# Scattering expert results to token order as each block ends, in a 16-expert stage on one Trainium2 core

## The chip, the cores and the metric

The kernel runs on one core of one Trainium2 chip. The metric is device time in microseconds (us) of one execution of the whole program; before the change it is 1019.32 us, the median of three runs (1016.58 to 1019.96).

## The reference, cut to what matters

The program is a chain of eight stages on 1024 tokens (4 sequences of 256) of 256 channels. The fourth of them is a mixture of experts: 16 experts of which each token uses two, and a shared expert that all use. Cut to that stage, with `x` the normalized tokens:

```python
probs = softmax(xt @ Wr.T + bias)
topk_val, topk_idx = top_k(probs, 2)
w = topk_val / (sum(topk_val) + 1e-9)
g = einsum('th,ehi->tei', xt, Wg)          # 16 experts, h = 256, i = 128
u = einsum('th,ehi->tei', xt, Wu)
y = einsum('tei,eih->teh', silu(g) * u, Wd)
oh = one_hot(topk_idx, 16)
routed = einsum('tke,tk,teh->th', oh, w, y)
shared = silu(xt @ sWg) * (xt @ sWu) @ sWd
```

The result, times a gate, is added to the token stream.

## The kernel before, in words

The kernel computes only the two chosen experts of each token. `sparse_moe` (L1279) first routes: VectorE finds each token's two experts and, with counts from TensorE, gives each of the 2048 (token, choice) pairs a slot. The slots of one expert are padded to whole blocks of 128, so there are NB = 31 blocks at most; `sloti` holds the slot of each pair. A product with one-hot matrices (L1425) turns this around: for each block and each of its 128 rows it gives the token's place within its tile (`ps[:, 6, 0:32]`) and the tile number (`ps[:, 6, 32:64]`), from which L1571 and L1572 make `rowid`.

The normalized tokens are stored to `h_rows` in HBM (L1333). POOL then issues one indexed DMA per block (L1352), which gathers 128 rows of 1 KB into one of NG = 4 buffers `xg`. A gather waits until TensorE has turned the block that used the buffer before (`s_xTp`).

The blocks run as a pipeline written out by hand. In step i TensorE turns block i (`turn_rows`, L1435), multiplies block i-1 with its expert's gate and up weights (`gate_up`, L1446), turns the hidden rows of block i-2 (L1455) and multiplies those of block i-3 with the down weights (L1468). ScalarE copies the turned rows (L1382) and takes silu (L1389). VectorE multiplies gate and up (`gated`, L1578), copies the turned hidden rows (`keep_hidden`, L1586), and copies the block's result rows into one of NY = 4 buffers `yo` (`keep_rows`, L1593). Between these, VectorE quantizes the weights of a later stage (L983 to L1002, 16 pieces). After the 31 blocks the same steps run for the NS = 8 token tiles of the shared expert, whose results VectorE adds to `x` at once (`add_shared`, L1598).

SP stores each block's result rows to `y_rows` in HBM (L1337) in the order of slots; `keep_rows` waits for the store of four blocks before (`s_st`). When all 31 stores have landed, POOL issues 16 more gathers (L1358), one per token tile and choice, which bring the two result rows of each token into `yk`. VectorE then adds them, each times its weight (L1617, L1619), tile by tile in the order of the gathers.

At the end of its list TensorE turns the quantized weights (`turn_w5`, L1031, L1037) and ScalarE copies them out of PSUM (`keep_w5`, L1043, L1045). The next stage starts when all engines have come to the end of this one.

Order within an engine is the order of the program; `v.link` issues a VectorE instruction and waits for it, `v.mark` issues it alone. Semaphores go up by 16 per DMA.

Of the kernel before, what the change touches and what calls it, by code (L numbers as in the profile page):

```python
# [10 lines left out]
P = 128  # L11
B, S, D, C = 4, 256, 256, 128
T = B * S
NT = T // P
# [6 lines left out]
ALU = mybir.AluOpType  # L21
ACT = mybir.ActivationFunctionType
AX = mybir.AxisListType
F32 = mybir.dt.float32
BF16 = mybir.dt.bfloat16
U16 = mybir.dt.uint16
U32 = mybir.dt.uint32
I32 = mybir.dt.int32
# [23 lines left out]
def build(nc, a, out):  # L52
    with ExitStack() as ctx:
        def sb(name, shape, dt=F32):
            return ctx.enter_context(nc.sbuf_tensor(name, shape, dt))
# [4 lines left out]
        def sem(name):  # L60
            held.append(nc.alloc_semaphore(name=name))
            return held[-1]
# [10 lines left out]
        ps = ctx.enter_context(nc.psum_tensor("ps", [P, 8, 512], F32))  # L73
# [10 lines left out]
        iota = sb("iota", [P, P])  # L84
        pcol = sb("pcol", [P, 1])
# [9 lines left out]
        g8 = sb("g8", [P, 8])  # L95
        rt3, rt7 = sb("rt3", [P, KD, 16]), sb("rt7", [P, KD, 8])
        h_rows = nc.dram_tensor("h_rows", (T, D), F32).ap()
        y_rows = nc.dram_tensor("y_rows", (31 * P, D), F32).ap()
        bias3 = sb("bias3", [P, 16])
        WORDS_B = WORDS_C = 13056  # L100
        low = ExitStack()
# [908 lines left out]
        def load_w5(sp, raw5):  # L1010
            sp.dma_start(raw5[:, 0, :], a["L2_W1"]).then_inc(s_w5, 16)
            sp.dma_start(raw5[:, 1, :], a["L2_W2"]).then_inc(s_w5, 16)
# [266 lines left out]
        def sparse_moe(tag, E, F, NB, W, WE, router, gate_col, s_weights, loads, ar, shared=False, bias=None,  # L1279
# [6 lines left out]
            NG, NY = 4, 4  # L1286
# [12 lines left out]
            sloti, blki = ar.take([2, NT], I32), ar.take([2, NT], I32)  # L1299
# [1 line left out]
            ohb = ar.take([NR, 32])  # L1301
            tokr = ar.take([NR, 2, 32], BF16)
            low_id = ar.take([32])
            rowid = ar.take([32], U32)
            le = ar.take([32, E])
            eb, ebi = ar.take([32]), ar.take([32], I32)
            xg = ar.take([NG, D])
# [3 lines left out]
            yo = ar.take([NY, D])  # L1311
            yk = ar.take([2, NT, D])
# [7 lines left out]
                 "xTp xT gu sil itm iTp iT y yo x").split())  # L1320
            s_got = [sem(f"{tag}_got{i}") for i in range(NG)]
            s_st = [sem(f"{tag}_stored{i}") for i in range(NY)]
            s_yk = [sem(f"{tag}_yk{i}") for i in range(NT)]
            over = lambda v: v.unsqueeze(2).broadcast_to([P, NT, E])
            xrows = out.rearrange("b (h p) d -> p (b h) d", p=P)
            with nc.Block(tag) as block:
                @block.sync
                def _(sp):
                    if with_w5:
                        load_w5(sp, raw5)  # L1330
                    for i in range(2):
                        sp.wait_ge(s_h, NT // 2 * (i + 1))
                        sp.dma_start(h_rows.rearrange("(t p) d -> p t d", p=P)[:, i * NT // 2:(i + 1) * NT // 2, :],  # L1333
                                     h[:, i * NT // 2:(i + 1) * NT // 2, :]).then_inc(s_hrow, 16)
                    for b in range(NB):
                        sp.wait_ge(s_yo, b + 1)
                        sp.dma_start(y_rows[b * P:(b + 1) * P, :], yo[:, b % NY, :]).then_inc(s_st[b % NY], 16)  # L1337
                    if store:
                        for hf in range(2):
                            sp.wait_ge(s_x, NS + TPH * (hf + 1))  # L1340
                            sp.dma_start(xrows[:, hf * TPH:(hf + 1) * TPH, :],
                                         x[:, hf * TPH:(hf + 1) * TPH, :]).then_inc(s_out, 16)
                        sp.wait_ge(s_out, 32)

                @block.gpsimd
                def _(pool):
                    pool.wait_ge(s_hrow, 32)
                    pool.wait_ge(s_rid, 1)
                    for b in range(NB):
                        if b >= NG:  # L1350
                            pool.wait_ge(s_xTp, b - NG + 1)
                        nc.gpsimd.indirect_dma_start(xg[:, b % NG, :], None, h_rows,  # L1352
                                                     bass.IndirectOffsetOnAxis(rowid[:, b:b + 1], 0)).then_inc(s_got[b % NG], 16)
                    for j in range(NY):
                        pool.wait_ge(s_st[j], 16 * len(range(j, NB, NY)))
                    for t in range(NT):
                        for k in range(2):
                            nc.gpsimd.indirect_dma_start(yk[:, k, t, :], None, y_rows[0:NB * P, :],  # L1358
                                                         bass.IndirectOffsetOnAxis(sloti[:, k, t:t + 1].bitcast(U32), 0)
                                                         ).then_inc(s_yk[t], 16)  # L1360

                def block_banks(u):

# [125 lines left out]
                def _(dve):  # L1489
                    v = Steps(dve, s_v)  # L1490
                    norm_on_vector(dve, v, s_var, s_sd, s_h)
                    nc.vector.tensor_scalar(tri[:, :], iota[:, :], pcol[:, 0:1], None, ALU.is_gt).then_inc(s_unit, 1)
                    nc.vector.memset(ones[:, :], 1.0).then_inc(s_unit, 1)
                    nc.vector.memset(unit, 1.0).then_inc(s_unit, 1)

# [61 lines left out]
                    for k in range(2):  # L1557
                        o = slice(k * NT, (k + 1) * NT)
                        ins = nc.vector.tensor_tensor(tokr[:, o, 1, :], ohb[:, o, :],
                                                      iota[:, 0:NT].unsqueeze(2).broadcast_to([P, NT, 32]), ALU.mult)  # L1560
                    ins.then_inc(s_tokr, 1)
                    for k in range(2):
                        nc.vector.tensor_tensor(ohr[:, k * NT:(k + 1) * NT, :], iota[:, :].unsqueeze(1).broadcast_to([P, NT, P]),
# [4 lines left out]
                    v.link(nc.vector.tensor_reduce(eb, le, AX.X, ALU.add))  # L1568
                    nc.vector.tensor_scalar(ebi, eb, float(E - 1), float(WE), ALU.min, ALU.mult).then_inc(s_eb, 1)
                    dve.wait_ge(s_inv, 1)  # L1570
                    v.link(nc.vector.tensor_copy(low_id, ps[:, 6, 0:32]))  # L1571
                    nc.vector.scalar_tensor_tensor(rowid, ps[:, 6, 32:64], float(P), low_id, ALU.mult, ALU.add).then_inc(s_rid, 1)  # L1572

                    def gated(u):
                        dve.wait_ge(s_sil, u + 1)
# [35 lines left out]
                        if with_w5:  # L1611
                            quantize_w5(dve, v, i, raw5, wq5, tmp5, am5, s_wq)
                    for t in range(NT):
                        dve.wait_ge(s_yk[t], 32)
                        if shared:
                            dve.wait_ge(s_x, t + 1)
                        v.link(nc.vector.scalar_tensor_tensor(x[:, t, :], yk[:, 0, t, :], wk[:, t, 0:1], x[:, t, :],  # L1617
                                                              ALU.mult, ALU.add))
                        nc.vector.scalar_tensor_tensor(x[:, t, :], yk[:, 1, t, :], wk[:, t, 1:2], x[:, t, :],  # L1619
                                                       ALU.mult, ALU.add).then_inc(s_x, 1)  # L1620

        def stage3():
            sparse_moe("stage3", NE3, P, NB3, W3, UW3, rt3, 5, s_w3, 7, Arena(regA, regC), shared=True, bias=bias3,
                       with_w5=True)
# [722 lines left out]
```

## Time and profile before

| | us |
|---|---|
| median of 3 runs | 1019.32 |
| lowest and highest run | 1016.58, 1019.96 |
| the profiled execution, its own time | 1017.64 |
| its span in the trace | 1015.9 |
| VectorE busy in the span | 728.4 (72%) |
| TensorE matmuls busy | 675.2 (66%) |
| ScalarE busy | 331.4 (33%) |
| POOL busy | 193.8 (19%) |

The span is the time from the first to the last instruction of the profiled execution. Busy times are sums over all eight stages, each of which has another limit, so they don't say what the stage in question is worth; that is read from the trace of its own stretch, 441 to 542 us. An indexed DMA on POOL shows as a busy POOL while its descriptors are made; the data lands later. PE is TensorE, DVE VectorE, ACT ScalarE, and SPq the queue of SP's DMAs.

### The profile page before, as it was taken

The numbers are of one execution on the slowest core, as the hardware profiler recorded it, in microseconds if no ns is written. First come the engines' busy times: TensorE is split into PE (matmuls) and PEld (weight loads), VectorE is DVE, ScalarE is ACT, GpSimd is POOL, SyncE is SP. The second block draws the span as 40 slices with busy tenths as digits, with TensorE's granted clock in tenths as the row PEclk, the third lists the DMA queues.
The fourth block names the chain that finished last, engine by engine and source line by source line (L and its number), as shares of the span: only waits on it lengthen the run. The fifth ranks groups of instructions, "written<-read, shape, count | busy, mean of one in ns | idle before, by whom it ended". The sixth has DMA issues, their size and how long they took to land. (4 is left out here: it accounts for less than half of the span.)

```text
span 1015.9 us, 9504 instructions
## 1 busy us (share of the span) xinstructions
PE 675.2 (66%) x3066; PEld 442.1 (44%) x3069; DVE 728.4 (72%) x1418; ACT 331.4 (33%) x530; POOL 193.8 (19%) x167
## 2 busy tenths in 40 slices
PE   4418986777777354349963454999990344389997
PEld 2304543343343243335742243556550123277775
DVE  5987798999999767659653783766429886944554
ACT  4004424525350133122302324555530222423231
POOL 0000002212222000034352940000003132203342
PEclk9759999999999776569986855999995575569999
DMA  9200004555555840323632000000005000000000
GB/s 243 76 12 0 1 0 78 87 94 93 97 90 97 206 128 1 124 62 108 133 92 87 0 1 0 1 2 1 1 1 207 0 1 0 10 0 1 20 3 21
DMA packets 35746, 55.27 MB, mean 54 GB/s; under 512 B 4578, under 2 KB 23658, under 8 KB 34418
## 3 DMA queue, kind: packets, MB, share of 16 engines
q0 software_dynamic: 10960, 22.94, 12.5%
q1 hardware_dynamic: 24738, 31.73, 10.2%
q8 instruction: 25, 0.41, 0.2%
q14 instruction: 23, 0.19, 0.1%
HBM read 31.73 MB, written 6.16 MB: 37 GB/s over the span
## 5 line engine op out<-in xcount | busy, mean ns | idle before, releaser
L499 PE MATMUL ps<-hT,regA 128*128 128x512 f32 x256 | 116.8, 599 | 1.3 <-ACT hT L424 1.3
L669 POOL DMA_DIRECT2D yssm<-regB x32 | 38.7, 1210 | 294.6 <-DVE regB L621 210.8
L613 DVE TENSOR_TENSOR_SCAN regB<-regB 128x512 f32<-128x512 f32 x64 | 74.9, 1212 | 5.0 <-DVE regB L608 0.5
L510 PE MATMUL ps<-regA,regC 128*128 128x256 f32 x256 | 64.8, 398 | 20.5 <-DVE regC L628 17.2
L1914 PE MATMUL ps<-regC 128*34 128x256 f32 x256 | 68.2, 389 | 11.6 <-ACT regC L1794 11.6
L499 PEld LDWEIGHTS ps<-hT,regA 128*128 128x128 f32 x256 | 49.2, 193 | 52.2 <-issue 47.7
L510 PEld LDWEIGHTS ps<-regA,regC 128*128 128x128 f32 x256 | 49.7, 199 | 39.8 <-DVE regC L628 27.1
L434 ACT ACTIVATE regC<-ps 128x512 f32<-128x512 f32 x32 | 19.1, 597 | 138.1 <-PE ps L499 138.0
L1128 POOL TENSOR_TENSOR w_lo<-regA,w_hi 128x768 fp32r<-128x768 f32 x22 | 42.4, 1932 | 100.3 <-ACT w_hi L1090 100.3
L1352 POOL DMA_INDIRECT regA<-h_rows,regA x31 | 29.5, 951 | 137.4 <-DVE regA L1572 107.1
L1266 DVE TENSOR_TENSOR regB<-regB,ps 128x512 f32<-128x512 f32 x22 | 15.1, 687 | 45.9 <-ACT regB L1108 45.9
L2036 DVE RECIPROCAL regC<-ps 128x8 f32<-128x8 f32 x32 | 6.6, 207 | 57.4 <-PE ps L1922 57.3
L1794 ACT ACTIVATE regC<-ps 128x512 f32<-128x512 f32 x64 | 38.1, 596 | 26.4 <-PE ps L1900 25.3
L621 DVE TENSOR_TENSOR regB<-regB,ps 128x512 f32<-128x512 f32 x64 | 41.1, 684 | 6.9 <-DVE regB L613 6.4
L456 PE MATMUL ps<-regC 96*128 96x512 bf16 x64 | 23.0, 387 | 31.7 <-DVE regB L621 19.8
L408 ACT ACTIVATE regB<-regC 128x510 f32<-128x510 f32 x64 | 40.2, 707 | 6.0 <-DVEq L647 5.9
L1858 PE MATMUL ps<-ident,regA 128*128 128x128 f32 x192 | 29.4, 318 | 17.7 <-DVE regA L2012 13.6
L608 DVE TENSOR_TENSOR regB<-regC,ps 128x512 f32<-128x512 f32 x64 | 40.9, 680 | 0.0
L2021 DVE TENSOR_REDUCE regC<-ps 128x4 f32<-128x960 f32 x64 | 40.3, 685 | 0.0
L2114 POOL TENSOR_TENSOR h<-h,regB 128x512 f32<-128x512 f32 x4 | 5.2, 1291 | 181.8 <-DVE h L156 181.8
L173 PE MATMUL ps<-ident,h 128*128 128x128 f32 x112 | 19.7, 350 | 28.0 <-DVE h L156 27.2
L1914 PEld LDWEIGHTS ps<-regC 128*34 128x34 f32 x256 | 23.6, 112 | 33.8 <-ACT regC L1794 12.5
(365 smaller groups left out, 1701.7 us busy)
## 6 DMA issues: line engine op xcount, KB each, us to landing
yssm<-regB POOLq DMA_DIRECT2D x32, 512.0 KB, 5.0
regB<-in_L_w SPq DMA_DIRECT2D x4, 1088.0 KB, 12.1
regA<-in_L_w SPq DMA_DIRECT2D x1, 4224.0 KB, 14.9
y_rows<-regA SPq DMA_DIRECT2D x31, 128.0 KB
regB<-in_L_w SPq DMA_DIRECT2D x1, 2176.0 KB, 13.1
regC<-in_L_W SPq DMA_DIRECT2D x2, 1024.0 KB, 5.7
x<-in_x SPq DMA_DIRECT2D x1, 1024.0 KB, 5.7
regB<-in_L_gate_pk SPq DMA_DIRECT2D x1, 1024.0 KB, 8.0
```

Source lines behind the costliest of these rows:

```text
L408: nc.scalar.activation(dA[:, g % RD, k, :, 1:S], src, ACT.Exp, scale=alog[:, k, n:n + 1]).then_inc(s_dA, 1)
L499: m = nc.tensor.matmul(ps[:, 2 + 2 * (u % 2) + j, :], w[:, k * 2048 + c * P:k * 2048 + (c + 1) * P], hT[:, k, hf * HALF:(hf + 1) * HALF], ...
L510: m = nc.tensor.matmul(ps[:, t // 2, (t % 2) * D:(t % 2 + 1) * D], itm[:, u % 2, t * P:(t + 1) * P], WDv[:, c // 2, c % 2, :], start=(c == ...
L608: v.mark(nc.vector.tensor_tensor(dBu[:, k, :], half(du, k, hf), ps[:, 6, :], ALU.mult))
L613: v.mark(nc.vector.tensor_tensor_scan(hs[:, k, :], dA[:, g % RD, k].rearrange("p b l -> p (b l)"), dBu[:, k, :], 0.0, ALU.mult, ALU.add))
L621: ins = nc.vector.tensor_tensor(hc[:, g % 2, k, :], hs[:, k, :], ps[:, 7, :], ALU.mult)
L669: nc.gpsimd.dma_start(y, hc[:, g % 2], accum_op=ALU.add).then_inc(s_y, 16)
L1128: nc.gpsimd.tensor_tensor(wP[LO][:, u % RING, :], W[:, u % NC, :], wP[HI][:, u % RING, :].bitcast(F32), ALU.subtract).then_inc(s_wL, 1)
L1352: nc.gpsimd.indirect_dma_start(xg[:, b % NG, :], None, h_rows, bass.IndirectOffsetOnAxis(rowid[:, b:b + 1], 0)).then_inc(s_got[b % NG], 16)
L1794: nc.scalar.activation(prob[:, n % 4, :], ps[:, 4 + n % 2, :], ACT.Exp, scale=SCALE4).then_inc(s_p, 1)
L1914: m = nc.tensor.matmul(ps[0:VW, 6 + j % 2, (n % 2) * S:(n % 2 + 1) * S], vaug[:, 2 * b + kt, hd, :], prob[:, n % 4, kt * S:(kt + 1) * S], ...
L2021: nc.vector.tensor_reduce(dst[:, :, :, j], sc[:, :, :, lo:hi], AX.X, ALU.max, negate=True).then_inc(s_mx, 1)
```

## The change

Result rows no longer go to slot order and come back by gathers. Each block's rows are written by an indexed DMA on POOL straight to a row that belongs to the token and choice: `y_rows` gets 2 x 1024 further rows, first those of choice 0 in token order, then those of choice 1. Rows of a block that no token uses go to a row of the old part. The tile number that the one-hot product carries is therefore counted from NB (31) up, plus 8 for the second choice, so that it is also the target's row number divided by 128, and 0 marks an unused row. Six VectorE instructions make from it `outid` (the target row) and `rowid` (the token, by masking).

POOL's list now holds both kinds of indexed DMA: gather i, then, from i = 8 on, the scatter of block i - 8, which waits for `keep_rows` of that block. SP stores nothing in the blocks; it waits until all scatters have landed and issues eight plain loads of two token tiles each, choice 0 and 1 in turn. VectorE waits for one pair of loads per two tiles.

```diff
-        y_rows = nc.dram_tensor("y_rows", (31 * P, D), F32).ap()
+        y_rows = nc.dram_tensor("y_rows", (31 * P + 2 * T, D), F32).ap()
...
-            rowid = ar.take([32], U32)
+            rowid, outid = ar.take([32], U32), ar.take([32], U32)
+            slot_f, slot_i, unused, spare = ar.take([32]), ar.take([32], I32), ar.take([32]), ar.take([32])
...
-            s_yk = [sem(f"{tag}_yk{i}") for i in range(NT)]
+            s_yk = [sem(f"{tag}_yk{i}") for i in range(NT // 2)]
...
-                    for b in range(NB):
-                        sp.wait_ge(s_yo, b + 1)
-                        sp.dma_start(y_rows[b * P:(b + 1) * P, :], yo[:, b % NY, :]).then_inc(s_st[b % NY], 16)
+                    for j in range(NY):
+                        sp.wait_ge(s_st[j], 16 * len(range(j, NB, NY)))
+                    for i in range(NT // 2):
+                        for k in range(2):
+                            r = NB * P + k * T + 2 * i * P
+                            sp.dma_start(yk[:, k, 2 * i:2 * i + 2, :],
+                                         y_rows[r:r + 2 * P, :].rearrange("(t p) d -> p t d", p=P)).then_inc(s_yk[i], 16)
...
-                    for b in range(NB):
-                        if b >= NG:
-                            pool.wait_ge(s_xTp, b - NG + 1)
-                        nc.gpsimd.indirect_dma_start(xg[:, b % NG, :], None, h_rows,
-                                                     bass.IndirectOffsetOnAxis(rowid[:, b:b + 1], 0)).then_inc(s_got[b % NG], 16)
-                    for j in range(NY):
-                        pool.wait_ge(s_st[j], 16 * len(range(j, NB, NY)))
-                    for t in range(NT):
-                        for k in range(2):
-                            nc.gpsimd.indirect_dma_start(yk[:, k, t, :], None, y_rows[0:NB * P, :],
-                                                         bass.IndirectOffsetOnAxis(sloti[:, k, t:t + 1].bitcast(U32), 0)
-                                                         ).then_inc(s_yk[t], 16)
+                    LAG = 2 * NG
+                    for i in range(NB + LAG):
+                        if i < NB:
+                            if i >= NG:
+                                pool.wait_ge(s_xTp, i - NG + 1)
+                            nc.gpsimd.indirect_dma_start(xg[:, i % NG, :], None, h_rows,
+                                                         bass.IndirectOffsetOnAxis(rowid[:, i:i + 1], 0)
+                                                         ).then_inc(s_got[i % NG], 16)
+                        if i >= LAG:
+                            b = i - LAG
+                            pool.wait_ge(s_yo, b + 1)
+                            nc.gpsimd.indirect_dma_start(y_rows, bass.IndirectOffsetOnAxis(outid[:, b:b + 1], 0),
+                                                         yo[:, b % NY, :], None).then_inc(s_st[b % NY], 16)
...
+                    v.link(nc.vector.tensor_scalar(spare, iota[:, 0:32], float(P), pcol[:, 0:1], ALU.mult, ALU.add))
...
                         ins = nc.vector.tensor_tensor(tokr[:, o, 1, :], ohb[:, o, :],
-                                                      iota[:, 0:NT].unsqueeze(2).broadcast_to([P, NT, 32]), ALU.mult)
+                                                      iota[:, NB + k * NT:NB + (k + 1) * NT].unsqueeze(2)
+                                                      .broadcast_to([P, NT, 32]), ALU.mult)
...
-                    v.link(nc.vector.tensor_copy(low_id, ps[:, 6, 0:32]))
-                    nc.vector.scalar_tensor_tensor(rowid, ps[:, 6, 32:64], float(P), low_id, ALU.mult, ALU.add).then_inc(s_rid, 1)
+                    v.link(nc.vector.scalar_tensor_tensor(unused, ps[:, 6, 32:64], 0.0, spare, ALU.is_equal, ALU.mult))
+                    v.link(nc.vector.tensor_tensor(low_id, ps[:, 6, 0:32], unused, ALU.add))
+                    v.link(nc.vector.scalar_tensor_tensor(slot_f, ps[:, 6, 32:64], float(P), low_id, ALU.mult, ALU.add))
+                    v.link(nc.vector.tensor_scalar(slot_i, slot_f, float(-NB * P % T), None, ALU.add))
+                    v.mark(nc.vector.tensor_copy(outid, slot_f))
+                    nc.vector.tensor_scalar(rowid.bitcast(I32), slot_i, T - 1, None, ALU.bitwise_and).then_inc(s_rid, 1)
+                    v.settle()
...
-                        dve.wait_ge(s_yk[t], 32)
+                        dve.wait_ge(s_yk[t // 2], 32)
```

## Rows read from the trace of the kernel before

**Rows 1.** Stretches: length, busy of each engine (instructions), granted clock, DMA share, GB/s.

```profile
452.00:482.00 30.00, 27.15 (x120) 17.23 (x118) 28.94 (x83) 8.44 (x26) 12.28 (x13) 1.00 0.40 111
482.00:500.00 18.00, 17.01 (x86) 12.81 (x86) 12.14 (x39) 6.22 (x19) 8.75 (x10) 1.00 0.63 131
500.00:512.00 12.00, 12.00 (x65) 10.20 (x64) 6.42 (x24) 3.71 (x12) 0.69 (x1) 1.00 0.59 122
```

**Rows 2.** Line L1352, the gathers of the blocks: durations, and what POOL waited for.

```profile
L1352 POOL DMA_INDIRECT regA<-h_rows,regA x31: 942/944/1079, 440.9 to 499.7; - x31
...
  PE ps L1435: 27.5, 23
```

**Rows 3.** Timeline of POOL: gathers 8, 29 and 30, and the first closing gather.

```profile
452.41 0.94 POOL L1352 DMA_INDIRECT regA<-h_rows,regA  x1 [0.90 <-PE ps L1435]
...
498.12 0.94 POOL L1352 DMA_INDIRECT regA<-h_rows,regA  x1 [0.68 <-PE ps L1435]
499.75 0.94 POOL L1352 DMA_INDIRECT regA<-h_rows,regA  x1 [0.68 <-PE ps L1435]
514.78 0.94 POOL L1358 DMA_INDIRECT regA<-y_rows,regA  x1 [14.09 <-DMA y_rows<-regA]
```

**Rows 4.** Line L1358, the closing gathers: durations, and idle time between them.

```profile
L1358 POOL DMA_INDIRECT regA<-y_rows,regA x16: 942/946/1132, 514.8 to 533.8; - x16
...
  issue: 4.6, 15
```

**Rows 5.** Timeline of the closing sum and of the end of the stage.

```profile
525.17 0.48 DVE L1617 SCALAR_TENSOR_TENSOR x<-regA,x 128x256 f32<-128x256 f32 x1
...
526.08 0.48 DVE L1617 SCALAR_TENSOR_TENSOR x<-regA,x 128x256 f32<-128x256 f32 x1
...
537.08 0.48 DVE L1619 SCALAR_TENSOR_TENSOR x<-regA,x 128x256 f32<-128x256 f32 x1
537.59 1.86 ACT L1043 COPY W1q<-ps 128x2048 bf16<-128x2048 bf16 x1 [17.76 <-remote]
539.35 1.87 ACT L1045 COPY W2q<-ps 128x2048 bf16<-128x2048 bf16 x1
```

**Rows 6.** Waits between 400 and 545: total us, times, longest.

```profile
ACT W1q L1043 <- remote: 17.8, 1, 17.8
...
DVE x L1617 <- DMA regA<-y_rows,regA: 4.7, 3, 1.7
...
DVE x L1598 <- PE ps L1468: 3.4, 2, 1.8
```

**Rows 7.** Timeline: the transposes that the first ScalarE copy reads.

```profile
523.19 1.06 PE L1031 MATMUL ps<-identb,regC 128*128 128x128 bf16 x16
```

**Rows 8.** Timeline of the head: row numbers, first gather, first use of it.

```profile
439.58 0.18 DVE L1571 COPY regA<-ps 128x32 f32<-128x32 f32 x1
439.80 0.19 DVE L1572 SCALAR_TENSOR_TENSOR regA<-ps,regA 128x32 uint32<-128x32 f32 x1
440.88 1.08 POOL L1352 DMA_INDIRECT regA<-h_rows,regA  x1 [107.11 <-DVE regA L1572]
...
443.86 0.69 PE L1435 MATMUL ps<-ident,regA 128*128 128x128 f32 x2 [5.06 <-DMA regA<-h_rows,regA]
```

**Rows 9.** SP's stores (line L1337), and two loads: KB each, us to landing.

```profile
L1337 SPq DMA_DIRECT2D y_rows<-regA x31: 319/320/333, 452.8 to 512.3; - x31
...
x<-in_x SPq DMA_DIRECT2D x1, 1024.0 KB, 5.7
...
regD<-in_q_wkv SPq DMA_DIRECT2D x1, 256.0 KB, 2.8
```

**Rows 10.** POOL's plain DMA out of SBUF in an earlier stage, and its landing.

```profile
L669 POOL DMA_DIRECT2D yssm<-regB x32: 1192/1201/1467, 154.8 to 332.6; - x32
...
DMA to landing us min/median/max: 5.0/5.0/5.6
```

**Rows 11.** Timeline: block 30 turned, a product and two result copies behind it.

```profile
505.60 0.38 PE L1435 MATMUL ps<-ident,regA 128*128 128x128 f32 x2
...
507.20 0.29 DVE L1578 TENSOR_TENSOR regA<-regA,ps 128x128 f32<-128x128 f32 x1 [0.67 <-ACT regA L1389]
...
507.60 0.41 DVE L1593 COPY regA<-ps 128x256 f32<-128x256 f32 x1
...
511.82 0.41 DVE L1593 COPY regA<-ps 128x256 f32<-128x256 f32 x1
```

## The prediction

> **What bounds the kernel now.** I read the table of stretches first, then the two groups of indexed DMAs on POOL, then the timeline of the stage's three seams (first gather, last block, closing sum).
>
> The 16-expert stage runs 31 expert blocks between about 441 and 512 us. While the second-layer weights are quantized beside the blocks, VectorE is full: 28.94 of 30 us. Later TensorE is: 17.01 of 18, then 12.00 of 12, at a granted clock of 1.00 [rows 1]. POOL is never full. Its 31 gathers take 0.94 us each, and it sits idle 27.5 us over 23 waits for TensorE to free a row buffer [rows 2]. From gather 8 (452.41) to gather 30 (499.75) the 22 blocks take 47.34 us, 2.15 a block [rows 3]; the last two gathers are 1.63 apart.
>
> After the blocks POOL waits 14.09 us for the last stored block and starts the closing gathers at 514.78 [rows 3]. These are 16 instructions of 0.946 us with 4.6 us of idle time over 15 gaps, so one every 1.25 us: POOL's own pitch with nothing to wait for [rows 4]. VectorE starts the weighted sum at 525.17, at 0.91 us a tile (to 526.08), and ends at 537.57 instead of after eight such tiles, because it waits 4.7 us for gathers [rows 5, 6]. Only then, at 537.59, does ScalarE copy the turned weights; both copies end at 541.22 and the stage closes [rows 5]. TensorE's transposes for the first copy stand at 523.19 to 524.25 [rows 7]. What kept ScalarE 17.8 us is given only as "remote" [rows 6].
>
> **The change, part by part.**
>
> *Head.* The two instructions after the inverse permutation become six, linked, before the row numbers are ready. Links stand 0.22 us apart (439.58 to 439.80) [rows 8], so four more cost 0.9 us. POOL's first gather and everything behind it wait for this: +0.9. The extra instruction beside the constants runs while VectorE waits for the router's logits: nothing, at worst 0.2. The token matrices keep their sizes: nothing.
>
> *Blocks.* SP's 31 stores leave a queue that did nothing else (0.32 us each [rows 9]): no gain on the path. POOL gets 31 scatters. From gather 8 on it alternates gather i and scatter i-8. A scatter's cost isn't in this trace. The nearest row is the gather: same 128 rows of 1 KB, indices on the other side. I take its 1.25 pitch. The upper bound is POOL's plain DMA from SBUF, 1.20 us long [rows 10], pitch 1.50. The lower bound is that POOL never binds.
>
> At 1.25 a pair needs 2.50 us where a block took 2.15, so POOL becomes the bound. Gather 8 moves to 453.3 (the head's 0.9), and gather 30 starts at 453.3 + 22 x 2.50 = 508.3 instead of 499.75. Before, gather 30 had slack: the first gather ends at 441.96 and TensorE uses it at 443.86, so 1.9 us to use [rows 8]. Gather 30 was therefore usable at 499.75 + 0.94 + 1.9 = 502.6 and TensorE took it at 505.60 [rows 11]. After, it is usable at 508.3 + 2.84 = 511.1: block 30 moves by 5.5 us. The eight shared tiles behind it keep their pace, so the start of the sum moves from 525.17 to 530.7.
>
> *The scatter's landing and the wait on it.* VectorE's copy into the ring of four result buffers now waits for the scatter of four blocks before. If gather u+4 starts at S, scatter u-4 lands at S + 1.25 + 0.94 + 1.9 = S + 4.1, taking the gather's 1.9. The copy's natural place is 2.0 us after gather u+3 is used (block 30 turned at 505.60, the rows of block 27 copied at 507.60 [rows 11]), at S - 2.5 + 2.84 + 2.0 = S + 2.3. So VectorE waits about 1.8 us per block. Behind it in VectorE's queue is the gating product of block u+3, whose natural place is 1.6 us (to 507.20) after block u+4 is used, S + 2.84 + 1.6 = S + 4.4. It starts near S + 4.1 + 0.41 = S + 4.5 instead and ends at S + 4.8. TensorE turns that product no sooner than after turning block u+5, usable at S + 5.3, so 0.5 us are to spare: nothing. A landing 2.2 us later (5.0 us from issue for the plain DMA [rows 10], against 2.84) would cost at most 1.7, once and not per block. An earlier landing gains nothing.
>
> *Tail.* The 16 closing gathers go, and with them 4.7 us of waits. Instead POOL drains: scatter 22 starts at 509.55, the other eight at 1.25 each, scatter 30 at 519.55, landed and seen by 519.55 + 0.94 + 1.9 = 522.4. Its rows are copied by 511.82 + 0.41 + 5.5 = 517.7, in time [rows 11]. SP then issues eight loads of 256 KB. Such a load lands after 2.8 us, 1024 KB after 5.7, so each further 256 KB takes 0.97 us [rows 9]. The four pairs are in by 526.2, 528.1, 530.1 and 532.0. The sum starts at 530.7 and needs the last pair at 530.7 + 6 x 0.91 = 536.2. So the loads are hidden; if one pair took 4 us longer the sum would feel it. Eight tiles without waits take 7 x 0.91 + 1.0 = 7.4 us: VectorE ends at 538.1 where it ended at 537.57.
>
> *Sum.* The sum starts 5.5 us later and is 5.0 us shorter: +0.5 us. Nothing after the stage changes, and I leave ScalarE's copies behind VectorE's end, as the row has them. 1017.64 + 0.5 = 1018.1. The profiled execution lies 1.7 under the median of 1019.32 and inside the runs' spread, so I don't shift the number, but let the range cover the 1.7.
>
> **Rivals.** A measurement of this kernel tells about 0.3% (3.06 us) from no change.
>
> *A: ScalarE's copies come loose (faster).* They start 13 us after the transposes they read, for a reason that the profile doesn't name. If that reason belongs to the closing gathers, which are the one thing special to those microseconds, the two copies run beside the sum. The stage then ends at 538.1 rather than 541.2 + 0.5, 3.6 us less: -3.1. If VectorE's two waits on TensorE in the shared tiles (3.4 us [rows 6]) have the same cause they go too: -6.5, 1011.1. For it: nothing on record but time separates transposes and copy. Against it: the first copy starts 0.02 us after VectorE's last instruction, as if tied to that, and that end stays.
>
> *B: the scatter is dearer on POOL (slower).* At the upper pitch of 1.50, 22 blocks lose another 22 x 0.25 = 5.5 us: +6.0, 1023.6. It decides from the point where 0.5 + 22 x (p - 1.25) passes 3.06, at p = 1.37, a scatter of 1.07 us. For it: every pair pays it, with no idle time left on POOL. Against it: 47 indexed DMAs here take 0.94 us at the median.
>
> *C: VectorE holds POOL up (slower).* If POOL could not write its descriptors while VectorE works, scatters put among the quantizing instructions would stretch. The rows speak against it: the gathers beside a VectorE that is 96% busy range from 0.942 to 1.079 us, the closing ones to 1.132 [rows 1, 2, 4]. Were every scatter as long as that longest one, 22 x 0.19 = 4.2 us would come on top: +4.7, 1022.3. The Trainium skill, page "SBUF — State Buffer", section "SBUF: two separate sides", states such a lock: a DVE instruction in a two-port mode shuts GpSimd out, whose DMA waits for descriptors (its figures: 620 ns alone, 3100 ns beside a copy). By it, as an estimate from that page, 22 scatters would lose up to 55 us; the trace doesn't show such a lock for the gathers.
>
> *D: POOL doesn't bind (faster).* If a pair fits in 1.63 us, only the head's 0.9 is lost and 5.0 gained in the sum: -4.1, 1013.5. Against it is the 0.3 us gap that even an empty POOL leaves between two indexed DMAs [rows 4].
>
> **How the numbers follow.** Forecast 0.40, A 0.29, B 0.22 (0.02 of it below its deciding point, so no change), C 0.04, D 0.05. Faster: A and D, 0.34. Same: 0.42. Slower: 0.24. The predicted time is the forecast's, 1018.1. The range runs from A's far end, 1011, to B's 1023.6 plus the 1.7 of the median, rounded to 1025; it leaves out a far end of C and combinations such as A with D, under 2 in 10.
>
> **What would show it.** Right: POOL's indexed DMAs 1.25 us apart without a break from gather 8 to the last scatter, near 520; TensorE waiting for gathered rows in the late blocks, where it waits for none now; the sum starting near 530.7 with no wait for loads; the last of eight loads in before 533. Wrong: scatters of 1.07 us or more (B, C), ScalarE's copies beginning before VectorE's last tile (A), TensorE still full in the late blocks (D), or a granted clock below 1.00 in them, which would mean that its pauses on gathers cost it the clock.

## The result, and the profile after

The change makes the kernel slower: median 1028.93 us (1027.31 to 1029.85, 4 runs) against 1019.64 us, ratio 1.0096, 95% interval 1.0072 to 1.0120. The profiled execution took 1028.65 us, its span is 1026.8 us, 10.9 more than before. The 10.9 split up so: the stage begins 1.2 us later for work ahead of it that the change doesn't touch; its head is 0.75 longer (from VectorE's search for the two experts to the first gather, 14.26 to 15.01); from the first gather to the next stage's first step it takes 111.2 us where it took 102.0, 9.2 more; behind it 0.2 less. All else lies in those 9.2.

The table of stretches, with the columns of [rows 1]:

```profile
452.00:482.00 30.00, 22.83 (x95) 13.61 (x93) 23.42 (x67) 6.38 (x21) 20.32 (x20) 1.00 0.28 89
482.00:500.00 18.00, 14.87 (x60) 9.97 (x60) 13.02 (x38) 3.53 (x11) 12.85 (x13) 0.91 0.27 88
500.00:512.00 12.00, 7.81 (x36) 5.36 (x36) 3.65 (x13) 2.78 (x9) 8.46 (x9) 0.97 0.31 97
512.00:525.00 13.00, 10.84 (x39) 7.65 (x39) 4.60 (x17) 3.05 (x10) 7.13 (x9) 0.76 0.24 83
525.00:545.00 20.00, 19.77 (x99) 16.04 (x99) 11.19 (x39) 3.80 (x13) 6.71 (x7) 0.91 0.41 134
```

In these stretches no engine is full any more until 525: VectorE fell from 28.94 to 23.42 of 30 us, TensorE from 12.00 to 7.81 of 12. POOL is the busiest newcomer, but not full either (20.32 of 30), and the DMA engines carry less than before (0.28 against 0.40). TensorE's granted clock, 1.00 throughout in [rows 1], falls below it behind pauses of TensorE: from 512 to 518 us it is 0.50, the lower of its two levels (1.2 and 2.4 GHz), behind three microseconds (509 to 512) in which TensorE was busy for 1.12.

POOL's two lines, then its timeline at gather 8, around one break, at gather 30 and at the last scatter:

```profile
L1365 POOL DMA_INDIRECT y_rows<-regA x31 | 32.1, 1034 | 14.2 <-issue 8.3 <-DVE regA L1606 5.9
L1359 POOL DMA_INDIRECT regA<-h_rows,regA x31 | 30.5, 982 | 127.3 <-DVE regA L1584 110.5 <-remote 7.8 <-issue 6.7
```

```profile
454.41 0.94 POOL L1359 DMA_INDIRECT regA<-h_rows,regA  x1 [1.68 <-PE ps L1441]
...
509.88 0.97 POOL L1359 DMA_INDIRECT regA<-h_rows,regA  x1 [0.30 <-issue]
511.15 1.00 POOL L1365 DMA_INDIRECT y_rows<-regA  x1 [0.30 <-issue]
513.95 0.96 POOL L1359 DMA_INDIRECT regA<-h_rows,regA  x1 [1.80 <-remote]
...
519.09 0.97 POOL L1359 DMA_INDIRECT regA<-h_rows,regA  x1 [0.30 <-issue]
...
535.35 0.97 POOL L1365 DMA_INDIRECT y_rows<-regA  x1 [0.43 <-issue]
```

A gather and a scatter take 2.57 us together, but every fourth pair POOL stops: at gathers 12, 16, 20, 24 and 28 it waits 1.40 to 1.80 us, 7.8 in all, put down to "remote". Gathers 8 to 30 stand 64.7 us apart, 2.94 a block (2.15 before).

What POOL waits for there is that TensorE has turned an earlier block. That had been done for long. Here is all engines' timeline around gather 16, and then the same two steps in the kernel before:

```profile
474.76 0.41 PE L1441 MATMUL ps<-ident,regA 128*128 128x128 f32 x2
475.01 1.10 PE L1452 MATMUL ps<-regB,regA 128*128 x4
...
477.27 0.29 DVE L1599 COPY regA<-ps 128x128 f32<-128x128 f32 x1 [1.49 <-PE ps L1461]
477.70 0.69 PE L1474 MATMUL ps<-regB,regA 128*128 x2 [1.48 <-DVE regA L1599]
478.03 0.42 DVE L1606 COPY regA<-ps 128x256 f32<-128x256 f32 x1 [0.47 <-remote]
478.07 0.37 ACT L1388 COPY regA<-ps 128x256 f32<-128x256 f32 x1 [2.67 <-remote]
478.31 0.96 POOL L1359 DMA_INDIRECT regA<-h_rows,regA  x1 [1.46 <-remote]
478.34 0.28 ACT L1395 ACTIVATE regA<-ps 128x128 f32<-128x128 f32 x1
```

```profile
475.02 0.41 PE L1435 MATMUL ps<-ident,regA 128*128 128x128 f32 x2
...
475.47 0.37 ACT L1382 COPY regA<-ps 128x256 f32<-128x256 f32 x1 [1.41 <-PE ps L1435]
```

In the kernel after, the transposes end at 475.17 and ScalarE's copy of them starts at 478.07: 2.90 us late. In the kernel before it follows 0.04 us behind their end. VectorE, which waits for another result of TensorE, and ScalarE and POOL, which both wait for these transposes, all come free between 478.03 and 478.31. The other way there is no delay: VectorE's copy ends at 477.56 and TensorE uses it at 477.70. So TensorE's results, and only its, become visible late and in lumps.

The trace also keeps records of when a semaphore went up. Of 122 by TensorE between 436 and 545 us, 31 stand more than 1 us behind the instruction that raised it, up to 6.0; of VectorE's 126 and ScalarE's 48 none is more than 0.02 us behind.

In each of the five breaks the result that POOL waits for comes 1.15 to 1.54 us after POOL's last indexed DMA has ended, so while POOL stands still. POOL stops because its four row buffers wait for TensorE, and its stop may be what lets the results out; no run tests that.

The end of the stage:

```profile
544.97 0.48 DVE L1630 SCALAR_TENSOR_TENSOR x<-regA,x 128x256 f32<-128x256 f32 x1
...
551.89 0.48 DVE L1632 SCALAR_TENSOR_TENSOR x<-regA,x 128x256 f32<-128x256 f32 x1
554.01 2.38 DVE L143 BATCH_NORM_STATS2 lnst<-x 128x6 f32<-128x256 f32 x7 [1.63 <-PEq L66]
```

```profile
545.46 1.87 ACT L1043 COPY W1q<-ps 128x2048 bf16<-128x2048 bf16 x1 [2.79 <-PE ps L1031]
547.22 1.87 ACT L1045 COPY W2q<-ps 128x2048 bf16<-128x2048 bf16 x1
```

The sum starts 19.8 us later than in [rows 5], takes 7.4 us in place of 12.4, and ScalarE's copies now run beside it, so that the next stage follows VectorE after 1.64 us instead of 5.28. 19.8 - 5.0 - 3.65 = 11.1, the 10.9 of the span.

### The profile page after: what moved, and what is told of

The parts are those of the page before. It is cut to its first block and busy times, and to the rows that moved or that the text cites. A ratio compares the mean times of both kernels' runs of the same rounds, so it can differ in the third digit from the quotient of the medians.

```text
span 1026.8 us, 9502 instructions
## 1 busy us (share of the span) xinstructions
PE 683.3 (67%) x3066; PEld 445.7 (43%) x3069; DVE 729.8 (71%) x1423; ACT 330.4 (32%) x530; POOL 211.2 (21%) x182
## 5 line engine op out<-in xcount | busy, mean ns | idle before, releaser
L510 PE MATMUL ps<-regA,regC 128*128 128x256 f32 x256 | 62.2, 386 | 22.1 <-DVE regC L628 19.0
L1452 PE MATMUL ps<-regB,regA 128*128 x124 | 37.5, 429 | 2.0 <-ACT regA L1388 2.0
```

The source lines that it names most:

```text
L510: m = nc.tensor.matmul(ps[:, t // 2, (t % 2) * D:(t % 2 + 1) * D], itm[:, u % 2, t * P:(t + 1) * P], WDv[:, c // 2, c % 2, :], start=(c == ...
```

## The experiments

Theory 1: POOL's issue alone is the bound. Theory 2: TensorE's results are held back while indexed DMAs follow each other closely. Theory 3: it is the scatter's direction. Theory 4: it is the ring of four result buffers. Each ratio is to the kernel before on the same chip, with its 95% interval. "8 to 30" is the time between these gathers, "stretch" that from the first indexed DMA to the next stage, both in the profiled execution.

| run | ratio | 8 to 30 | stretch |
|---|---|---|---|
| before | 1 | 47.3 | 102.0 |
| after | 1.0096 (1.0072 to 1.0120) | 64.7 | 111.2 |
| e1 dummy gathers | 1.0199 (1.0150 to 1.0247) | 64.4 | 120.4 |
| e2 plain stores | 0.9920 (0.9903 to 0.9936) | 47.5 | 90.3 |
| e3 scatters alone | 0.9889 (0.9866 to 0.9913) | | |
| e4 eight row buffers | 1.0074 (1.0058 to 1.0091) | 63.9 | 108.2 |
| e5 plain extra loads | 0.9995 (0.9978 to 1.0012) | 47.5 | 106.5 |
| e6 few rows | 1.0182 (1.0160 to 1.0204) | 65.9 | 120.0 |
| e8 busy POOL | 1.0014 (1.0002 to 1.0026) | 51.1 | 104.4 |
| e9 half as many | 1.0064 (1.0040 to 1.0087) | 50.5 | 109.1 |
| e13 POOL's plain DMAs | 0.9982 (0.9965 to 0.9999) | 48.3 | 102.2 |
| e10 paced closing | 1.0038 (1.0021 to 1.0055) | 47.2 | 105.0 |
| e7 turn early | 1.0046 (1.0030 to 1.0063) | 47.1 | 107.4 |
| e11 first five paced | 0.9986 (0.9973 to 0.9999) | 47.3 | 102.1 |
| e12 after, paced | 1.0065 (1.0042 to 1.0087) | 67.3 | 111.1 |
| e14 the same, eight buffers | 1.0104 (1.0068 to 1.0139) | 68.5 | 112.2 |
| e15 paced closer | 1.0096 (1.0068 to 1.0124) | 66.1 | 112.2 |

### Density or direction: e1, e2, e3, e4

e1, on the kernel before:

```diff
                         nc.gpsimd.indirect_dma_start(xg[:, b % NG, :], None, h_rows,
                                                      bass.IndirectOffsetOnAxis(rowid[:, b:b + 1], 0)).then_inc(s_got[b % NG], 16)
+                        if b >= 2 * NG:
+                            n = b - 2 * NG
...
+                            nc.gpsimd.indirect_dma_start(yk[:, 0, n % 8, :], None, h_rows,
+                                                         bass.IndirectOffsetOnAxis(rowid[:, b:b + 1], 0)).then_inc(s_xx[n % 8], 16)
```

> The kernel before, with one more gather behind each of the gathers 8 to 30 (23 in all), which reads the same rows into a buffer that nobody reads; no scatter, plain stores as before. So the POOL queue issues indexed DMAs as densely as in the kernel after, in one direction only. Theory 1 (POOL's issue alone): a pair takes 2.57 us, the queue runs without a break, gather 30 is issued near 453.3 + 22 x 2.57 = 509.8 (499.75 before), and the time is near 1026. Theory 2 (TensorE's results reach the others late while indexed DMAs are issued close together, of whatever direction): results of TensorE are late by 2 us and more every fourth block, POOL waits on a turn of rows at gathers 12, 16, 20 and so on, gather 30 is issued past 515, and the time is 1030 to 1042. Theory 3 (the scatter's direction, its writes to HBM) and theory 4 (the ring of four result buffers, whose scatters land too late): no late results here, as theory 1: near 1026.

Measured: 1035.90 us, without a single scatter. POOL's and ScalarE's waits between 453 and 512 us:

```profile
POOL regA L1353 <- remote: 5.0, 3, 2.0
...
ACT regA L1398 <- remote: 7.8, 2, 3.9
...
ACT regA L1391 <- remote: 6.1, 3, 2.6
```

POOL stops for 1.25 to 2.0 us at gathers 12, 15, 19, 22, 26 and 29, and gather 30 starts at 516.02. Theory 2 holds; theories 1, 3 and 4 asked for 1026 and an unbroken queue.

e2, on the kernel after:

```diff
+sp.dma_start(y_rows[b * P:(b + 1) * P, :], yo[:, b % NY, :]).then_inc(s_st[b % NY], 16)
...
-r = NB * P + k * T + 2 * i * P
+r = k * T + 2 * i * P
...
-nc.gpsimd.indirect_dma_start(y_rows, bass.IndirectOffsetOnAxis(outid[:, b:b + 1], 0),
-                             yo[:, b % NY, :], None).then_inc(s_st[b % NY], 16)
```

> The kernel after, with the scatters replaced by the kernel before's plain stores in block order and the loads of the end reading rows of those in place of token order (so the rows are not put back into token order: that part of the computation is left out). Head and tail of the change alone. All four theories that blame the blocks: gathers 8 to 30 take 47 us as before, the closing sum begins near 526 and takes 7.4 us, ScalarE's copies run beside it, and the time is 1019.6 + 0.9 - 5.0 - 3.65 = 1011.9 (1009 to 1015). Rival (the six linked steps of the head, or the loads of the end, are what lost the time): 1017 or more.

Measured: 1008.27 us, 8.9 under the 1017.17 of before, where 7.75 was expected (1008.27 lies just below the range). Head and tail alone are a gain, of the terms worked out: the sum takes 7.4 us and the copies stand beside it. One term more shows: the sum starts 81.27 us behind the first gather, 84.29 before, because VectorE's waits on TensorE in the shared tiles (3.4 us [rows 6]) are down to 0.2.

e3, on the kernel after:

```diff
+r = (b * P) % T
+sp.dma_start(xg[:, b % NG, :], h_rows[r:r + P, :]).then_inc(s_got[b % NG], 16)
...
-nc.gpsimd.indirect_dma_start(xg[:, i % NG, :], None, h_rows,
-                             bass.IndirectOffsetOnAxis(rowid[:, i:i + 1], 0)
-                             ).then_inc(s_got[i % NG], 16)
```

> The kernel after, with each block's gather replaced by a plain load of 128 rows by SP (so the rows are not brought into expert order: that part is left out); the 31 scatters stay. POOL issues one indexed DMA per block, as in the kernel before, but a scatter. Theory 2 (density): no late results of TensorE, blocks at 2.15 us, time near 1012 (1008 to 1016). Theory 3 (direction): late results every eighth scatter or more often, 1018 or more. Theory 4 (ring of four): VectorE's row copies wait for scatters now and then; 1012 to 1018. Theory 1: as theory 2.

Measured: 1006.46 us, a little below the range of theory 2. With 31 scatters and nothing else indexed every copy of ScalarE follows its transposes by 0.04 us. With e1, where gathers alone made results late, theory 3 falls. Scatters alone at the dense pitch were not run.

e4, on the kernel after:

```diff
-            NG, NY = 4, 4
+            NG, NY = 4, 8
```

> The kernel after, with eight result-row buffers in place of four, so that a row copy waits for a scatter eight blocks back, which is always in. Theory 4 (ring of four): the stalls every fourth block go, gather 30 is issued near 510, the closing sum begins near 534, and the time is near 1018. Theories 2 and 3: POOL goes on waiting every fourth block, sum start near 545, time 1027 to 1031. Theory 1: 1027 to 1031 too, but with POOL unbroken.

Measured: 1024.57 us, a little under the range of theory 2 (the before measured beside it is 2.5 lower than that of the result; the two ratios overlap). POOL's waits stay ("remote" 7.5 us in the stage, 7.8 in the kernel after), gather 30 starts 63.9 us behind gather 8. Theory 4 falls.

### What about an indexed DMA: e5, e6, e8, e9, e13

All five are the kernel before with something else in the place of e1's dummies; e5 has it on SP, behind the store of block b:

```diff
+sp.dma_start(yk[:, 0, b % 8, :], h_rows[r:r + P, :]).then_inc(s_xx[b % 8], 16)
```

> The kernel before, with 23 more plain loads of 128 rows of 1 KB, one behind each of SP's first 23 stores of result rows, into a buffer that nobody reads: the same extra rows as in the run with dummy gathers, but by SP and not indexed. Theory 2 (indexed DMAs close together hold TensorE's results back): no late results, 31 blocks as in the kernel before, time within 2 us of it. Theory 6 (it is the traffic of the DMA engines, whoever orders it): late results every few blocks as with the dummy gathers, 1025 or more.

Measured: 1017.60 against 1017.57 us, no late result in the blocks. In the profiled execution TensorE waited once, for 2.1 us, for gathered rows where the kernel before doesn't, and the stretch is 4.6 us longer, but the median isn't. This traffic doesn't hold TensorE's results.

```diff
+nc.gpsimd.indirect_dma_start(yk[0:32, 0, n % 8, :], None, h_rows,
+                             bass.IndirectOffsetOnAxis(rowid[0:32, b:b + 1], 0)).then_inc(s_xx[n % 8], 16)
```

> The kernel before with the 23 dummy gathers again, each of 32 rows in place of 128: as many indexed DMAs, a quarter of their rows. Theory 2a (the number of indexed DMAs in a stretch decides): late results as with full dummies, time 1028 to 1038. Theory 2b (the number of rows, that is of descriptors in flight, decides): at 160 rows per block instead of 256 hardly any late results, time 1016 to 1022.

Measured: 1036.74 us, as e1. A dummy of 32 rows costs POOL as much as one of 128 (983 ns in the mean, 994 in e1), and holds TensorE as much. First its line, then ScalarE's wait between 453 and 512:

```profile
L1359 POOL DMA_INDIRECT regA<-h_rows,regA x23 | 22.6, 983 | 7.0 <-issue 7.0
```

```profile
ACT regA L1391 <- remote: 11.4, 4, 4.1
```

```diff
+nc.gpsimd.memset(yk[:, 0, 0:4, :], 0.0).then_inc(s_xx, 1)
```

> The kernel before, with a POOL memset of 128x1024 (0.94 us each in this kernel's trace) where the dummy gathers stood, behind each of the gathers 8 to 30. POOL is as busy as in the kernel after but issues no more DMAs. Theory 2: no late results; the pair takes 0.95 + 0.3 + 0.94 = 2.2 us, about the 2.15 of a block, so the time is within 3 us of before. Theory 7 (any work of POOL, not its DMAs, holds the others back): late results, 1025 or more.

Measured: 1018.85 us. POOL is as busy, but its waits between 453 and 512 are short and for work that has just ended:

```profile
POOL regA L1353 <- PE ps L1441: 6.3, 11, 1.0
POOL regA L1353 <- issue: 2.0, 12, 0.2
```

e9 against e1:

```diff
-                        if b >= 2 * NG:
+                        if b >= 2 * NG and b % 2 == 0:
```

> The kernel before, with a full dummy gather behind every second gather from 8 (12 in all): three indexed DMAs per two blocks. If late results begin at some density (theory 2 with a threshold between one per block, where there were none, and two per block, where they came every fourth block), fewer and shorter ones or none: 1017 to 1024. If each further indexed DMA costs alike: 1017 + 18.7 x 12 / 23 = 1027.

Measured: 1023.91 us, at the upper end of the first forecast. Results were late up to block 8, behind the first gathers (1.25 us apart) and the first dummies; then in time; then late again from block 19 on, where the quantizing is over, a block takes 1.63 us, and POOL issues without pause. POOL's timeline in the middle, where they were in time, and then where they were not:

```profile
484.14 0.95 POOL L1353 DMA_INDIRECT regA<-h_rows,regA  x1 [1.18 <-PE ps L1444]
485.39 0.95 POOL L1359 DMA_INDIRECT regA<-h_rows,regA  x1 [0.30 <-issue]
486.64 1.04 POOL L1353 DMA_INDIRECT regA<-h_rows,regA  x1 [0.30 <-issue]
488.85 0.94 POOL L1353 DMA_INDIRECT regA<-h_rows,regA  x1 [1.17 <-PE ps L1444]
...
501.10 0.94 POOL L1353 DMA_INDIRECT regA<-h_rows,regA  x1 [1.49 <-remote]
```

In the middle POOL issues three indexed DMAs 1.25 us apart and then stands still for 1.2 us. So a short pitch alone doesn't hold the results; it takes a longer run without a pause. The first six gathers of the kernel before say the same: they stand 1.25 to 1.39 us apart, and ScalarE's copies follow their transposes by at most 0.04 us.

```diff
+nc.gpsimd.dma_start(yk[0:32, 0, n % 8, :], h_rows[0:32, :]).then_inc(s_xx[n % 8], 16)
```

> The kernel before with the 23 dummies of 32 rows again, ordered by POOL in the same places but as plain DMAs (no index). Theory 2c (any DMA whose descriptors POOL writes holds TensorE's results back when they come close together): late results as with the indexed ones, 1025 to 1037, if POOL issues them as fast. Theory 2d (only indexed ones do, and these come once per block here): no late results, within 2 us of before.

Measured: 1015.82 us against 1018.02, no late results in the blocks. Its dummies, same rows, same queue, no index:

```profile
L1359 POOL DMA_DIRECT2D regA<-h_rows x23 | 12.9, 561 | 0.0
```

So neither traffic, nor rows, nor POOL's work, nor any POOL DMA of this size: it takes indexed DMAs close together. Whether the index itself does it isn't shown: a plain dummy also kept POOL for 561 ns where an indexed one of as many rows kept it for 983. The ratio of e13 is also a warning: a kernel from which nothing was taken measures 0.9982, and its stretch is no shorter.

### The same thing in the kernel before: e10, e7, e11

e10, on the kernel before (e11 has `1 <= 2 * t + k <= 5`):

```diff
                         for k in range(2):
+                            if 2 * t + k > 0:
...
+                                nc.gpsimd.memset(xg[:, 0:2, :], 0.0).then_inc(s_xx, 1)
                             nc.gpsimd.indirect_dma_start(yk[:, k, t, :], None, y_rows[0:NB * P, :],
```

> The kernel before, with a POOL memset of 128x512 (about 0.5 us) between its 16 closing gathers, so that they are some 1.8 us apart in place of 1.25. Theory 2 (density): TensorE's results come in time there, VectorE's waits on TensorE in the shared blocks (3.4 us) go, ScalarE's copies begin near 525 and not with the last gather; the last gather is some 8 us later, so VectorE ends near 545 and the next stage follows it by 1.6 us in place of 5.3: near 1021. Rival (the results wait for the end of the whole run of gathers, whatever its pace): the copies begin past 543, near 1025.

Measured: 1021.00 us. The copies, which began at 537.59 in [rows 5]:

```profile
521.59 1.86 ACT L1043 COPY W1q<-ps 128x2048 bf16<-128x2048 bf16 x1 [2.96 <-PE ps L1031]
523.35 1.87 ACT L1045 COPY W2q<-ps 128x2048 bf16<-128x2048 bf16 x1
```

With the closing gathers 1.65 us apart (1.8 was planned) the "remote" wait of [rows 6] is gone, and VectorE's waits on TensorE there are down to 0.2 us, as theory 2 asked. The time is longer, for the last gather is later.

e7, on the kernel before: TensorE's first half below (the second at i == NB + 6; ScalarE copies behind its activations of tiles NB + 2 and NB + 5).

```diff
+                        if with_w5 and i == NB + 3:
...
+                            for o in range(FF // P):
+                                for k in range(KD):
+                                    m = nc.tensor.transpose(psb[:, 6 + k, o * P:(o + 1) * P],
...
+                            m.then_inc(s_wqT, 1)
...
-                    if with_w5:
-                        turn_w5(pe, wq5, s_wq, s_wqT)
```

> The kernel before, with TensorE's turn of the next stage's quantized weights (32 transposes, lines 1031 and 1037) and ScalarE's two copies of them moved up among the shared-expert blocks, into PSUM banks 6 and 7, which are free there. If the copies ended the stage of before (they began at 537.59, when VectorE was done, and took 3.7 us): the next stage starts 1.6 us behind VectorE as in the kernel after, 3.65 us are won, near 1014 (1012.5 to 1015.5). Rival (the gap of 5.3 us between VectorE's end and the next stage has another cause): within 1 us of before.

Measured: 1022.40 us, slower, a miss. The next stage did follow VectorE after 1.65 us, but the second copy and the shared blocks' activations moved into the dense gathers and were caught there (the transposes of that copy ended at 521.13):

```profile
524.91 1.86 ACT L1404 COPY W2q<-ps 128x2048 bf16<-128x2048 bf16 x1 [4.90 <-remote]
...
534.79 0.28 ACT L1390 ACTIVATE regA<-ps 128x128 f32<-128x128 f32 x1 [7.49 <-remote]
```

The sum began at 541.04 instead of 525.17. A gap at the end was bought with a later start.

> The kernel before, with a POOL memset of 128x512 (0.54 us) behind each of the first five closing gathers alone, so that these are 1.65 us apart, as in the run with all of them paced, until TensorE has turned the next stage's weights, and the other ten 1.25 us apart as before. Theory 2 (density): VectorE's waits on TensorE go, ScalarE's copies begin near 522 as in that run; the last gather is 2.0 us later than in the kernel before, so VectorE ends 2.0 us later and the next stage follows after 1.6 to 2.7 us in place of 5.3: 0.6 to 1.7 us faster than before, ratio 0.998 to 0.9995. Rival (the results are late again as soon as the gathers are 1.25 us apart, before the copies are out): 2 us slower, ratio 1.002.

Measured: 1015.54 against 1017.16 us. The copies ran at 522.62 and 524.39 as expected, but the stretch is 102.1 us, no shorter than before's, and the ratio is no lower than that of e13. A gain over the kernel before isn't shown. No version here that does all of the work is measurably faster than it.

### How close is too close: e12, e14, e15

On the kernel after; e14 and e15 with eight result-row buffers:

```diff
                             if i >= NG:
                                 pool.wait_ge(s_xTp, i - NG + 1)
+                            if i >= LAG:
...
+                                nc.gpsimd.memset(yk[:, 0, 0, :], 0.0).then_inc(s_xx, 1)
...
                         if i >= LAG:
                             b = i - LAG
...
+                            nc.gpsimd.memset(yk[:, 0, 0, :], 0.0).then_inc(s_xx, 1)
                             pool.wait_ge(s_yo, b + 1)
```

> The kernel after, with a POOL memset of 128x256 (about 0.33 us) ahead of each gather from 8 on and of each scatter, so that indexed DMAs are issued some 1.48 us apart instead of 1.28. POOL has more work. Theory 2 with a threshold below 1.48: TensorE's results come in time, POOL runs without a break, a pair takes 2.96 us, as much as it took with the stalls, gather 30 is issued near 519 as before, but TensorE is not held: the last scatter is near 533, the closing sum begins near 541, and the time is 1021 to 1026, faster than the kernel after. Theory 2 with a threshold above 1.48, or theory 1 (POOL's issue is all): slower than the kernel after, 1031 to 1040.

Measured: 1022.34 us, in the range of theory 2 with the border below 1.48. From block 5 to the last, ScalarE copies every block 0.04 us behind its transposes, and most pairs on POOL take 2.97 us, without a break. But VectorE's row copies wait (453 to 545 us):

```profile
DVE regA L1614 <- DMA y_rows<-regA: 20.7, 13, 2.7
```

The stretch, 111.1, is that of the kernel after; the lower median isn't a gain in this stage, as the profile has it.

> The kernel after, paced as in the run before it of that kind (memsets of 128x256, a pitch of 1.48 us) and with eight result-row buffers, so that VectorE's row copies no longer wait for scatters (20.7 us of waits in the paced run with four). If these waits were on the path: the stretch from the first gather to the next stage is 106 to 109 us (111.1 in the paced run with four, 111.2 in the kernel after, 102.0 in the kernel before), the time 1018 to 1021. If the gathers, two pitches apart per block, set the pace alone (gather 30 at 79 us behind the first): 110 to 111.5, 1021 to 1024.

Measured: 1028.21 us, stretch 112.2, both above either forecast. The 20.7 us of waits are gone and nothing is won. From 453 to 512 no wait of POOL is above 0.2 us and none of ScalarE is "remote"; TensorE, between 482 and 528, waits for rows at nearly every block:

```profile
POOL regA L1365 <- issue: 3.2, 20, 0.2
...
ACT regA L1396 <- PE ps L1449: 30.1, 19, 2.3
```

```profile
PE ps L1449 <- DMA regA<-h_rows,regA: 16.2, 14, 1.6
```

This is theory 1 in its pure form: two pitches of 1.48 us a block, 22 x 2.97 = 65.3 us and the rest single longer issues.

> The same with memsets of 128x128 (about 0.2 us), a pitch of some 1.36 us. If TensorE's results come in time at that pitch too: gather 30 is 22 x 0.24 = 5.3 us earlier than with a pitch of 1.48, the stretch is 5 us shorter than in the run beside it, 1016 to 1019. If they are late again (the border lies between 1.36 and 1.48): POOL waits on turns of rows again, and the stretch is as long as or longer than in the run beside it.

Measured: 1026.14 us, stretch 112.2. At a pitch of 1.38 us (two in 2.76) the late results are back:

```profile
POOL regC L1364 <- remote: 2.3, 2, 1.3
...
ACT regA L1403 <- remote: 3.9, 1, 3.9
```

So in the blocks, where POOL has next to no pause, the border lies between 1.38 and 1.48 us. In the shared tiles of e12 and e14, behind gather 30, results came up to 3.5 us late at 1.47, so it is near there. On either side the stretch is 111 to 112 us: dense, TensorE is held; paced, TensorE waits for rows.

## Why the prediction was wrong

*What bounds the kernel:* right for the blocks. It left one row unexplained: "remote", 17.8 us [rows 6]. That row was the effect that decided, already present where 16 indexed DMAs stood 1.25 us apart; rival A tied it to the closing gathers, but no step asked what 62 such DMAs in the blocks would do.

*Head:* right, 0.75 us against 0.9.

*Blocks:* the failed step is "gather 30 starts at 453.3 + 22 x 2.50 = 508.3", with POOL taken as unbroken. The pitch was nearly right (2.57; a scatter has a median of 0.999 us, its mean 1.034). 22 x 2.57 = 56.5, but 64.7 were measured: the stalls at every fourth pair, 7.8 us or 6.3 beyond the usual gaps of 0.30, are most of the difference. TensorE waited for gathered rows nowhere behind gather 8, though such waits were named as a sign of being right. Nor did block 30 follow: it was turned at 528.44, not 2.84 us behind gather 30, because products, activations and row copies of the blocks before it were late too. The start of the sum moved by 19.8 us instead of 5.5. 1.2 of the difference is the later begin of the stage.

*The wait on the scatter:* no bound, as worked out, but the 1.8 us a block don't show either: VectorE's row copies waited for late results of TensorE alone (4.5 us in six waits). In the paced e12 they did wait for scatters. With eight buffers the stretch was 3.0 us shorter in the dense kernel, which the ratios of e4 and after don't separate, and no shorter in the paced one (e14).

*Tail:* right. 7.4 us without a wait for loads, which landed after 4.9 us in the median, later than the 2.8 and 0.97 taken, but inside the slack.

*ScalarE's copies left behind VectorE's end:* wrong. They came loose as rival A said (-3.65), and VectorE's waits on TensorE in the last shared tiles went too (3.4 to 0.2 us). Without the scatters A's terms make 0.9 - 5.0 - 3.65 = -7.75 us, or -11.15 with those waits; e2 measured 8.9 us under before, its stretch 11.7 under. In the changed kernel the blocks take that back about twice over.

*B, C, D:* B's deciding point (a scatter of 1.07 us) was not reached. C: scatters beside the quantizing took at most 1.23 us; the lock of which the Trainium skill tells (page "SBUF — State Buffer", section "SBUF: two separate sides") doesn't show here. The page ties it to VectorE instructions in a two-port mode, and no run tells which of these were. D: POOL does bind. Of the signs of being wrong, two came true: ScalarE's copies began before VectorE's last tile (A), and the granted clock fell below 1.00, though behind pauses for late results and not for gathers. The range missed the time by 4 us, since none of its cases held TensorE back.

## What to carry to other kernels

Count indexed DMAs, not bytes: here each needs about 1 us of POOL, whether it moves 32 rows or 128, and a long run of them beside a working TensorE needs some 1.5 us from one to the next, or pauses. Trading 16 of them at the end for 31 more in the middle loses what plain loads win. A wait that the profile can only call "remote" is a price whose cause is unknown: ask which operation stands around it, and whether the change adds more of that.

## What the runs showed of the hardware

Not expected: in a run of indexed DMAs on POOL 1.25 to 1.38 us apart, results of TensorE reach the other engines late, by up to some 6 us in the blocks (up to 11 in e7), several at once, while results of VectorE and ScalarE come in time. Plain DMAs of 561 ns on POOL don't do it (e13), and it needs neither the rows (e6), nor the scatter's direction (e1), nor the traffic (e5), nor a busy POOL (e8). At 1.65 us apart it is gone, at 1.48 in the blocks, and at 1.25 where POOL pauses for 1.2 us behind every third (e9). Why it strikes TensorE alone, and whether the index, POOL's time at it or the number of such DMAs under way decides, the runs don't tell. The granted clock averaged 0.76 in the stretch from 512 to 525, behind a pause of TensorE; what that cost wasn't measured apart, and e14, with the clock at 1.00 through the blocks, was no shorter.
